# Second edge pipeline of a fused graph kernel: 128 partitions in each indirect DMA in place of 125

## What is computed

```
edge_index = jnp.stack([src, dst])
x = _layernorm(x + _L0_gnn_ref(x, edge_index, edge_attr_128, ...))
x = _layernorm(x + _L1_gnn_ref(x, edge_index, ...))
x = _layernorm(x + _L2_gnn_ref(x, edge_attr_20, edge_weight, src, dst, ...))
x = _layernorm(x + _L3_gnn_ref(x, edge_index, ...))
```

```
h = x @ W_in2f
Wij = (shifted_softplus(f_ij @ W_f1 + b_f1) @ W_f2 + b_f2) * rcut_ij[:, None]
y = segment_sum(h[idx_j] * Wij, idx_i)
out = shifted_softplus(y @ W_o1 + b_o1) @ W_o2 + b_o2
```

## Time and profile before

| What | Value |
|---|---|
| median of 3 runs | 2379.52 us (2376.27 to 2380.89) |
| the profiled execution, its own time | 2378.39 us |
| its span, first to last instruction | 2376.7 us |
| mean granted TensorE clock | 0.949 of full speed |
| PE, DVE, ACT, POOL busy | 2084.7, 1991.1, 1783.7, 1518.7 us |
| gathers of sums (line 1846) | 100, 133.6 us busy |
| puts of final rows (line 1893) | 100, 134.5 us busy |

### The profile page before, as it was taken

How to read it: one execution, slowest core, us unless ns; L and a number is a source line. 1 busy time by engine, 2 the same in 40 slices (tenths; PEclk the granted TensorE clock), 3 DMA queues, 4 the chain that set the end, 5 groups by cost and what they waited for, 6 DMA issues and landing times. The chain is left out here.

```text
span 2376.7 us, 45628 instructions
## 1 busy us (share of the span) xinstructions
PE 2084.7 (88%) x14016; PEld 1740.5 (73%) x14016; DVE 1991.1 (84%) x2942; ACT 1783.7 (75%) x3691; POOL 1518.7 (64%) x1114
## 2 busy tenths in 40 slices
PE   5999999999998799997998788888699999486664
PEld 4999999999998577775776677777577776365563
DVE  7999999999997566666998799999699998498564
ACT  4889998989897577776776688888699998375221
POOL 6888766777730534340677788870188886688787
PEclk9999999999999899998999899999899999699776
DMA  4777666555665888886886788885477765786653
GB/s 111 149 168 160 157 163 171 163 158 157 180 182 178 206 254 255 255 252 180 207 214 142 165 197 194 195 206 143 115 195 203 197 195 160 167 210 163 166 162 99
DMA packets 322547, 427.40 MB, mean 180 GB/s; under 512 B 113683, under 2 KB 169589, under 8 KB 322308
## 3 DMA queue, kind: packets, MB, share of 16 engines
q1 hardware_dynamic: 210004, 367.20, 54.9%
q0 software_dynamic: 112000, 56.93, 14.2%
q10 hardware_dynamic: 304, 0.36, 0.0%
HBM read 239.24 MB, written 185.90 MB: 179 GB/s over the span
## 5 line engine op out<-in xcount | busy, mean ns | idle before, releaser
L1784 POOL DMA_INDIRECT acc<-combined,first_ x100 | 208.7, 2087 | 84.9 <-issue 39.9
L510 PE MATMUL banks<-mats,g_hT 128*125 128x256 f32 x1000 | 259.2, 382 | 0.0
L529 PE MATMUL banks<-mats,g_zT 128*125 128x128 f32 x2000 | 238.8, 273 | 0.0
L844 POOL DMA_INDIRECT gin_xs<-x,from_ x100 | 125.4, 1254 | 162.0 <-DMA x_of_src<-gin_xs 138.0
L529 PEld LDWEIGHTS banks<-mats,g_zT 128*125 128x125 f32 x2000 | 228.1, 188 | 0.0
L1846 POOL DMA_INDIRECT em_y<-acc,from_ x100 | 133.6, 1336 | 132.8 <-PE banks L1949 102.9
L510 PEld LDWEIGHTS banks<-mats,g_hT 128*125 128x125 f32 x1000 | 189.7, 190 | 28.4 <-issue 0.2
L1012 DVE TENSOR_TENSOR gin_acc<-gin_acc,gin_qr 125x512 f32<-125x512 f32 x125 | 86.6, 693 | 117.1 <-ACT gin_qr L974 117.1
L590 ACT ACTIVATE g_zT<-banks,cols 128x500 f32<-128x500 f32 x250 | 178.9, 776 | 2.6 <-PE banks L518 2.6
L573 ACT ACTIVATE g_sq<-banks 125x512 f32<-125x512 f32 x250 | 144.8, 590 | 43.2 <-PE banks L510 42.7
L437 POOL DMA_INDIRECT g_xd<-in_x,idx x100 | 124.0, 1240 | 72.8 <-PE banks L544 46.0
(11 more groups left out here) (408 smaller groups left out, 6609.6 us busy)
## 6 DMA issues: line engine op xcount, KB each, us to landing
acc<-g_zero SPq DMA_DIRECT2D x126, 224.0 KB
x<-g_x SPq DMA_DIRECT2D x125, 224.0 KB
g_x<-in_xT SPq DMA_DIRECT2D x100, 250.0 KB, 3.3
gin_x<-x SPq DMA_DIRECT2D x50, 448.0 KB
h<-gin_hr SPq DMA_DIRECT2D x50, 448.0 KB
al_h<-h SPq DMA_DIRECT2D x38, 448.0 KB
al_x<-x SPq DMA_DIRECT2D x38, 448.0 KB
out<-al_out SPq DMA_DIRECT2D x38, 448.0 KB
```

The costliest lines, as they stand in the source:

```text
L510: m = nc.tensor.matmul(bank[0:P, 256 * j:256 * j + 256], HT[q % 2][:, c:c + P], K.W1c, start=False, stop=j == 1)
L529: m = nc.tensor.matmul(pO[q % 2][0:P, D * j:D * j + D], ZT[q % 2][:, h, P * j:P * j + P], K.W2[:, h, :], start=False, stop=j == R - 1 and ...
L1784: pool.indirect_dma_start(out=K.acc, out_offset=bass.IndirectOffsetOnAxis(ap=K.first[:, g, r:r + 1], axis=0), in_=CR[:, g, r * D:r * D + D ...
```

## The change

Four tiles get 128 partitions in place of 125: `combined`, the buffers `em_y`, and the index tiles `from_` and `first_`. All other users see the first 125 partitions as before. The gathers of sums and the puts of final rows in the second edge pipeline now name all 128 partitions. So that the three further rows do no harm, DVE presets `from_` to 0 (row 0 is gathered into partitions that nothing reads) and `first_` to `NOWHERE` (100000, past the bound of 49,999), and POOL zeroes partitions 96 to 127 of `combined` at the start of `edges_first`, before ACT writes the real rows there; a semaphore `blank` orders the two, with a wait on POOL ahead of its rounds and one on ACT ahead of the first `keep_c`.

```
@@ setup
-    K.from_, K.first, K.of_h3, K.to_d, K.slot = [keep(n, [P, EG, R], I32) for n in (...)]
+    K.of_h3, K.to_d, K.slot = [keep(n, [P, EG, R], I32) for n in ("of_h3", "to_d", "d_slot")]
+    K.from_all, K.first_all = [keep(n, [128, EG, R], I32) for n in ("from_", "first_")]
+    K.from_, K.first = K.from_all[0:P], K.first_all[0:P]
...
                 link(nc.vector.tensor_tensor(K.ob[:, :], K.c("o0"), K.ob[:, :], ALU.subtract))
+                link(nc.vector.memset(K.from_all[:, :, :], 0))
+                link(nc.vector.memset(K.first_all[:, :, :], NOWHERE))
                 dve.wait_ge(idx_in, 16)
@@ edges_first, POOL
                 nc.gpsimd.iota(trash[:, :], ...).then_inc(tr, 1)
+                pool.wait_ge(tr, 3)
+                nc.gpsimd.memset(CR_all[96:128, :, :], 0.0).then_inc(blank, 1)
+                past(pool, blank, 0)
                 for k in range(rounds):
@@ edges_first, ACT
                 def keep_c(k):
                     past(act, cp, k)
+                    if k == 0:
+                        past(act, blank, 0)
@@ Inputs
-        self.X, self.XD, self.YD, self.Y = sb("x", 2), sb("xd", 3), sb("yd", 3), sb("y", 4)
+        self.X, self.XD, self.YD, self.Y_all = sb("x", 2), sb("xd", 3), sb("yd", 3), sb("y", 4, 128)
+        self.Y = [y[0:P] for y in self.Y_all]
...
-            pool.indirect_dma_start(out=self.Y[k % 4][:, r, :], out_offset=None, in_=self.K.acc,
-                                    in_offset=bass.IndirectOffsetOnAxis(ap=self.K.from_[:, k, r:r + 1], axis=0))...
+            pool.indirect_dma_start(out=self.Y_all[k % 4][:, r, :], out_offset=None, in_=self.K.acc,
+                                    in_offset=bass.IndirectOffsetOnAxis(ap=self.K.from_all[:, k, r:r + 1], axis=0))...
@@ edges_middle, put
-                        pool.indirect_dma_start(out=out, out_offset=bass.IndirectOffsetOnAxis(ap=K.first[:, k, r:r + 1], axis=0),
-                                                in_=C(k)[:, r, :], in_offset=None, bounds_check=N - 1,
+                        pool.indirect_dma_start(out=out, out_offset=bass.IndirectOffsetOnAxis(ap=K.first_all[:, k, r:r + 1], axis=0),
+                                                in_=ins.CR_all[:, k, r * D:r * D + D], in_offset=None, bounds_check=N - 1,
@@ program
-        CR = big.enter_context(nc.sbuf_tensor("combined", [P, EG, R * D], F32))
+        CR_all = big.enter_context(nc.sbuf_tensor("combined", [128, EG, R * D], F32))
+        CR = CR_all[0:P]
```

More of the change, by code:

```diff
@@ L151, in setup @@
     K.src, K.dst, nxt = idx[:, 0], idx[:, 1], idx[:, 2]
-    K.from_, K.first, K.of_h3, K.to_d, K.slot = [keep(n, [P, EG, R], I32) for n in ("from_", "first_", "of_h3", "to_d", "d_slot")]
+    K.of_h3, K.to_d, K.slot = [keep(n, [P, EG, R], I32) for n in ("of_h3", "to_d", "d_slot")]
+    K.from_all, K.first_all = [keep(n, [128, EG, R], I32) for n in ("from_", "first_")]
+    K.from_, K.first = K.from_all[0:P], K.first_all[0:P]
     K.c = lambda n: K.cols[:, K.col[n]:K.col[n] + 1]
@@ L1505, in _, with edges_first @@
                               (2, on(n.reduce_c, dve))])
-def edges_first(nc, K, CR, rounds, got_h):
-    name, last = "ef", EG - 1
+def edges_first(nc, K, CR_all, rounds, got_h):
+    name, last, CR = "ef", EG - 1, CR_all[0:P]
     ctx = ExitStack()
@@ L1533, in edges_first @@
         (hT, bt, back, a, rm, x2, x2T, xt, hp, scan, g1, ab, e1, l1, rl, sp_, wp, wt, mt, mT, mr, sc, sel, dl, df, fi, cp, cr, tr, added,
-         rows_a, rows_b) = [sem(n) for n in (
+         rows_a, rows_b, blank) = [sem(n) for n in (
             "hT", "bt", "back", "a", "rm", "x2", "x2T", "xt", "hp", "scan", "g1", "ab", "e1", "l1", "rl", "sp", "wp", "wt", "mt", "mT", "mr",
-            "sc", "sel", "dl", "df", "fi", "cp", "cr", "tr", "added", "rows_a", "rows_b")]
+            "sc", "sel", "dl", "df", "fi", "cp", "cr", "tr", "added", "rows_a", "rows_b", "blank")]
         with nc.Block() as block:
@@ L1824, in __init__, with sb @@
     def __init__(self, nc, K, CR, ctx):
-        def sb(n, k):
-            return [ctx.enter_context(nc.sbuf_tensor(f"em_{n}{i}", [P, R, D], F32)) for i in range(k)]
-        self.K, self.CR = K, CR
-        self.X, self.XD, self.YD, self.Y = sb("x", 2), sb("xd", 3), sb("yd", 3), sb("y", 4)
+        def sb(n, k, rows=P):
+            return [ctx.enter_context(nc.sbuf_tensor(f"em_{n}{i}", [rows, R, D], F32)) for i in range(k)]
+        self.K, self.CR_all, self.CR = K, CR, CR[0:P]
+        self.X, self.XD, self.YD, self.Y_all = sb("x", 2), sb("xd", 3), sb("yd", 3), sb("y", 4, 128)
+        self.Y = [y[0:P] for y in self.Y_all]
         self.IV = [ctx.enter_context(nc.sbuf_tensor(f"em_iv{i}", [128, G], F32)) for i in range(3)]
@@ L1845, in get @@
         for r in range(R):
-            pool.indirect_dma_start(out=self.Y[k % 4][:, r, :], out_offset=None, in_=self.K.acc,
-                                    in_offset=bass.IndirectOffsetOnAxis(ap=self.K.from_[:, k, r:r + 1], axis=0)).then_inc(self.got[k % 4], 16)
+            pool.indirect_dma_start(out=self.Y_all[k % 4][:, r, :], out_offset=None, in_=self.K.acc,
+                                    in_offset=bass.IndirectOffsetOnAxis(ap=self.K.from_all[:, k, r:r + 1], axis=0)).then_inc(self.got[k % 4], 16)
 def edges_middle(nc, K, out, ins):
@@ L2369, in program @@
         big = ExitStack()
-        CR = big.enter_context(nc.sbuf_tensor("combined", [P, EG, R * D], F32))
+        CR_all = big.enter_context(nc.sbuf_tensor("combined", [128, EG, R * D], F32))
+        CR = CR_all[0:P]
         ROUNDS, PAIRS = 10, NG // 2 - LATE
         got_h = K.lasting("h_got", 1)[0]
-        edges_first(nc, K, CR, ROUNDS, got_h)
+        edges_first(nc, K, CR_all, ROUNDS, got_h)
         K.end_phase()
-        ins = Inputs(nc, K, CR, big)
+        ins = Inputs(nc, K, CR_all, big)
         side, ahead = sums_and_gather(K, CR, ROUNDS, sem("added"), got_h, ins)
```

## The result

The changed kernel has a median of 2385.76 us (8 runs, 2380.56 to 2395.28) beside 2379.03 us for the kernel before (8 runs, 2374.49 to 2381.75). The ratio is 1.0036, with a 95% interval of 1.0021 to 1.0051: +8.6 us, between +5.0 and +12.1 (times 2380 us; the two medians alone lie 6.7 us apart). The forecast was 2376.8 us; the result lies above the range and on the other side of no change.

What follows compares the result with a forecast made beforehand. Compute, 12.61 us a round, was taken to bound the second edge pipeline, leaving POOL's 14.5 us tail to shorten. Terms -1.95, -0.45, -0.6 and +0.3 gave -2.7 us: 2375.7 profiled, 2376.8 median; range 2372.5 to 2381.0.

Steps and rivals of the forecast that it cites:

- POOL's tail: End of the second edge pipeline: 14.5 us from last multiply to next stage, the only part this change can shorten.
- the compute holds the rounds: Second edge pipeline: the compute keeps its 12.61 us a round, so rounds before the last put give nothing.
- the last put would be released by the multiply: End of the second edge pipeline: last put starts at 2022.6 in place of 2024.55, no longer behind the put before: -1.95 us.
- The landing: End of the second edge pipeline: the last put's data lands 0.6 us earlier, between 0 and 0.9.
- The price of a 128-row instruction: POOL's time for each gather or put of 128 rows: 0.11 us less, from 48 fewer packets at 2.4 ns.
- The last four puts: POOL's final instructions in the second edge pipeline, each 0.11 us shorter: -0.45 us.
- the cap by the compute: Second edge pipeline: once POOL's lag goes, the compute is late next, limiting the last put's earlier start to 1.95 us.
- The setup: Two added DVE memsets of 128x100 at the start, in full on the path: +0.3 us.
- One reading of the waits: POOL's five waits for landings, 18.7 us in all, were taken to lie mostly in the second edge pipeline's tail.
- rival C: First edge pipeline: POOL's long memset holds DVE and the stage behind it, +8.6 us, 2388.1 us; chance 0.08.
- the argument against it: First edge pipeline: line 1092 ran at 0.16 us inside line 1541's memset, so a POOL memset need not hold DVE.
- signs of being wrong: Tail after the last multiply stays near 14.5 us or falls below 9, or the first edge pipeline starts its transposes later.

Runs made afterwards that it cites:

- the later memset: The changed kernel with POOL's memset waiting until DVE has done its folding and two index conversions; ratio 1.0010 to the kernel before.
- the memset alone: The changed kernel with only POOL's memset and its waits left, gathers and puts at 125 rows again; ratio 1.0047 to the kernel before.
- the doubled one: The changed kernel with POOL's memset run twice, one behind the other; ratio 1.0071 to the kernel before.

## The prediction against the runs, step by step

**Right.** That only POOL's tail could gain, and that the compute holds the rounds: 300.3 us for 25 multiplies, and 300.5 before. That the last put would be released by the multiply, with a gain of 1.95 us there: measured 2.09. That a put emits 32 packets in place of 80. The landing, -0.6: measured -0.72.

**Mis-sized.** The price of a 128-row instruction was put at -0.11 us, between the bounds +0.03 and -0.73; a gather fell by 0.23 and a put by 0.27. If all of that went by the 48 packets, which no run separates from the rest, a packet would cost 4.7 to 5.6 ns and not the 2.4 taken from the accumulating puts. The last four puts gave 0.83 us for 0.45. It changed little, because the cap by the compute was right. The setup cost 0.53 us for 0.3. One reading of the waits was wrong, though nothing in the sum hung on it: of the 18.7 us that POOL waited for landings, 14.5 lie ahead of 2015 us, and only the last wait, 4.17 us, reaches into the tail.

**The step that failed: rival C and its 0.08.** The price was nearly right: a memset estimated at 11.3 us took 10.76 and held DVE for 9.5. The place was right too, the steps ahead of PE's line 1123. What failed is the argument against it: that line 1092 ran at 0.16 us inside line 1541's memset. That row shows that a memset doesn't hold a two-input step of one column, and I let it stand for the whole chain of lines 1095 to 1103. The last of that chain, line 1103, is of another kind: one input, SBUF to SBUF, 128 columns. No row of before shows such a step beside a POOL memset, but the trace of before has one beside another POOL instruction that only writes, an iota at the start of `gin`, and it wasn't looked for:

```profile
775.68 0.55 POOL L838 IOTA gin_place<- 25x500 f32 x1 [89.45 <-POOLq L113]
775.70 0.61 DVE L1039 TENSOR_SCALAR gin_neg<-ident 128x128 bf16<-128x128 f32 x1 [7.46 <-PEq L113]
```

It took 0.61 us and ended 0.085 us after the iota, just as the held scale ended 0.085 us after the memset; line 1103, of the same shape though with float32 output, took 0.285. (That the iota held it is argued from this; no run takes the iota away.) The step should have been bounded from both sides, 0 and the memset's length, and the range should have reached C. The rule that I weighed, the Trainium skill's "GPSIMD Engine Reference", section "Key points", has two halves, two SBUF inputs or a two-port mode; I held only the first against the trace. What the runs show is C as it would come by the other half: the later memset takes it away (1.0010), the memset alone brings it (1.0047), the doubled one holds the next such steps (1.0071). That C's total, +8.6 us, is also the measured difference is luck: C set a stall of 11.3 against a gain of 2.7, and the runs have a stall of 9.5, of which 7.9 stay in the stage, and no gain.

**The step that was missing: the stage's closing.** All that follows the last landing, 3.87 us before, I let stand. Of it 2.66 us were POOL's drain, and that became 7.89. Nothing in the rows of before shows that it could grow. The forecast would have been wrong without the memset as well: gathers and puts at 128 rows without the stall stand at 1.0010 and 1.0012, where the forecast's -2.7 us is 0.9989 (the second with the last group's puts at 125 rows).

Of what I named as signs of being wrong, two came: the tail didn't shrink (16.1 us), and the first edge pipeline starts its transposes later.

## What to carry to other kernels

Before a long fill goes to an idle POOL, go through every DVE instruction that can meet it, by kind: a row that shows one kind running undisturbed says nothing about another. The same fill a few us later cost nothing here, and a fill that comes with data that moves anyway needs no slot at all. When the instructions of an engine become faster and the engine has slack, look for the gain only where the engine ends last, and take that end down to the stage's closing instruction, which the views show as idle time.

## What the runs showed of the hardware that was not expected

- A POOL memset of 32x12800 (10.76 us) holds a DVE TENSOR_SCALAR of 128x128 from SBUF to SBUF until it ends: 9.80 us in place of 0.285; two conversions of 125x100, 9.52 and 9.44 in place of 0.21. Steps with two SBUF inputs (0.68 to 0.69 us for 500 or 512 columns), a reduction (0.69) and one-column steps, a TENSOR_SCALAR among them (0.15 to 0.16), run beside it at their usual time.
- An indirect DMA of 128 rows costs POOL 0.98 us at the end of the stage, one of 125 rows 1.19, and emits 32 packets in place of 80.
- POOL's closing drain took 2.7, 3.3, 5.0 or 7.9 us in the same stage, by which indirect DMAs ahead of it had 128 rows, although the last bytes had landed; a pause of 10.76 us ahead of it didn't shorten it. Its lengths differ by multiples of 0.327 us. Why is open.
